# Feed-forward norm and output projection by halves, the gate projection z at the end of the preceding pass, weights by one branch, and a new order of calls

## The chip, the cores and the metric

The kernel runs on 1 core of one Trainium2 chip. The metric is the device time in microseconds (us) of one execution, the median of several runs.

## The reference

Sixteen sequences of 512 tokens with 256 features pass through two layers. Layer 0 is attention and a feed-forward part, layer 1 a selective scan and a small quantised linear map. Each part stands behind a layer norm, with shift, scale and gate (`sa, ca, ga, sb, cb, gb`) from a conditioning vector.

```python
# layer 0
h = _layernorm(x) * (1 + ca) + sa
q, k, v = heads of h @ W.T (16 heads of 16), q and k normed per head
x = x + ga * (softmax(causal(q k^T / 4)) v) @ Wu.T
h = _layernorm(x) * (1 + cb) + sb
t = silu(tlin(h, w1)) * tlin(h, w2)            # 256 -> 1024
t = gelu(tlin(t, h1)); t = gelu(tlin(t, h2))   # 1024 -> 1024, twice
x = x + gb * tlin(t, w3)                       # 1024 -> 256
# layer 1
h = _layernorm(x) * (1 + ca) + sa
xp, z = split(h @ W_in)                        # 256 -> 2 x 512
dlt, Bm, Cm = split(xp @ W_xproj)
delta = clip(softplus(dlt @ W_dt + b_dt), 0.001, 0.1)
for each token: s = (1 + A * delta) * s + Bm * delta * xp; y = sum(Cm * s)   # 16 states
x = x + ga * ((y + D * xp) * silu(z)) @ W_out
h = _layernorm(x) * (1 + cb) + sb
x = x + gb * (quantise(h, blocks of 32) @ quantise(W).T + bias)
```

## The kernel before

**Passes.** One pass works on up to three sequences at once, in stages that the engines interleave. `att` and `ffn` are layer 0 of sequence b, `pre` is layer 1 up to the scans of states 0 to 11 for b-1, and `fin` is the rest of layer 1 for b-2: the scans of states 12 to 15, the gate, the output projection and the quantised linear map. `Pass` says which parts are on. The program is: a set-up; pass 0 (attention alone, which also splits the weights); the feed-forward of sequence 0 with pass 1; a loop of two turns over seven unrolled steady passes with all parts on (14 passes); and two last passes without layer 0. A steady pass begins here where the last feed-forward product `mid(17)` of the one before ends on PE.

**Order.** The order of the work on each engine is written out by hand, as a list of calls at the end of `tensor_pass`, `scalar_pass`, `vector_pass` and `gpsimd_pass`. Engines run their lists strictly in order and wait on semaphores, so a call that waits holds everything behind it. What depends on the part of the pass:

- *Attention*, four quads of heads with three groups each: `scores` (PE) to `find_max` (DVE, L1988) to `turn_max` (PE) to `shift_q` (DVE, L1995) to `scores_turned` (PE, L1131) to `exp_probs` (ACT, L1569) to `causal_probs` (POOL) to `values` (PE) to `row_sums`, `invert_sums`, `weigh` (DVE, L2000). `att_proj` (PE, L1162) and `att_add` (DVE) close it.
- *Gate projection z*: `gate_in(m)` (PE, L1006, four of two matmuls each), `gate_silu(m)` (ACT, L1521) into `z_s`, then `gate_out` (POOL, L714), which multiplies the scan's sum, and `out_proj` (PE, L1043). It reads the normed input `h3` of the pass before, so it has to stand ahead of `pre_affine`, which overwrites `h3`.
- *Layer 1*: `in_proj`, `x_proj`, `dt_proj` (PE), `dt_bias`, `softplus` (ACT), `clip_dt` (DVE, L2017), then for each state a decay (ACT), a product with B, a scan and a product with C (DVE), and an addition (POOL). States 12 to 15 are `tail_*`, 0 and 1 `head_*`, both beside the attention; 2 to 11 (`times_b`, `scan`, `times_c`) run beside the feed-forward.
- *Feed-forward norm*: `ffn_mean` (PE), `ffn_centre` (DVE, L229), `ffn_square` (ACT, L238), `ffn_var` (PE, L223), `ffn_rstd` (ACT, a Ln L242 and an Exp L244), `ffn_scale` (DVE, L233), `ffn_affine` (ACT, L1404: for each half of the features a value rounded to fp32r and a full one), `split_h` (POOL: the difference of the two). Each of centre, square and scale is one instruction over both halves.
- *Feed-forward*: every weight product is two fp32r matmuls (high and low part of the activations) of 0.23 us; `up(n)` waits for rounded and split input together. `up_gate` is a Silu (ACT, L1412), `gate_up` (DVE, L1940) the product, `gelu` (L1425).

**Weights.** Pass 0 rounds each of 22 weight tiles to fp32r (`split_act`), computes what rounding left (`split_dve`: a difference L451 and its largest value L453), and stores both, as `w_hi` and `w_lo`. `find_flag` then puts into `has_rest` whether anything was left. The weights of the reference are -1, 0 and 1, so nothing is. Each product asks `has_rest` by a branch (L918) of its own, 34 in a pass; the block that it jumps over holds 4 or 16 matmuls.

**Activation tables.** Silu, Gelu, and Ln with Exp stand in different table sets of ACT. `preload_act_table_set(LN_EXP)` at L1454 and L1523 loads the set that has both Ln and Exp; elsewhere the program gets a load where a function is not in the set that is loaded. A steady pass has five loads: before `gate_silu(0)`, after `gate_silu(3)`, before `up_gate(0)`, before `gelu(0)` and before `next_rstd`.

## Time and profile before

| | us |
|---|---|
| Median of 3 runs | 4162.34 (4157.99 to 4164.06) |
| The profiled execution, its own time | 4167.61 |
| Its span, first to last instruction | 4165.8 |
| PE busy, DVE busy | 3523.9 (85%), 3318.2 (80%) |
| POOL busy, ACT busy | 2716.0 (65%), 2583.4 (62%) |

The span is the time from the first to the last instruction. An engine's busy time is the sum of its instructions. In a timeline a row is one instruction or a run of equal ones: start and duration in us, the number behind x, and in brackets how long the engine stood idle before it and which work it waited for. An fp32 matmul shows as two rows of matmuls, so x4 is two matmuls. The steady passes follow each other every 235.5 us, and the rows below are from one of them.

### The profile page before, as it was taken

Reading aid. Unit: us, or ns where it says so; the run is one execution under the profiler, and the core shown is the slowest. Engines: PE = TensorE matmul, PEld = TensorE weight load, DVE = VectorE, ACT = ScalarE, POOL = GpSimd, SP = SyncE. Lnnn points to the kernel's source line nnn. Section 1 sums busy time; section 2 is a strip of 40 time slices with the busy share of each in tenths; the row PEclk is TensorE's granted clock in tenths of the full one; section 3 lists DMA queues with packets and bytes.
Section 4 is the critical chain, followed back from the end, with each engine's and each line's share of the span. In section 5 each row is a group of like instructions: output and inputs, shape, how many; then the busy total and the mean of one; then the engine's idle time right before and its main releaser. Section 6 shows DMA issues by size and latency. Waiting matters only on the chain. (4 is left out here: it accounts for less than half of the span.)

```text
span 4165.8 us, 50421 instructions
## 1 busy us (share of the span) xinstructions
PE 3523.9 (85%) x16621; PEld 2034.0 (49%) x16621; DVE 3318.2 (80%) x3646; ACT 2583.4 (62%) x3703; POOL 2716.0 (65%) x1960
## 2 busy tenths in 40 slices
PE   5687888989899998989898898989999898989513
PEld 3263645546373645546373554636364554636201
DVE  4514878989798888979797887979898897979694
ACT  2345566767667676766666676767667676666431
POOL 0132866768595876768595776759586776768563
PEclk9799999999999999999999999999999999999756
DMA  4630201102030301103030211203030211203000
GB/s 164 258 105 15 97 21 62 62 26 97 6 117 1 97 26 61 62 21 102 6 102 17 82 41 46 77 8 115 1 107 16 76 46 41 82 6 102 0 5 5
DMA packets 69435, 247.81 MB, mean 59 GB/s; under 512 B 9472, under 2 KB 10112, under 8 KB 68736
## 3 DMA queue, kind: packets, MB, share of 16 engines
q1 hardware_dynamic: 66816, 235.35, 16.8%
q10 hardware_dynamic: 2304, 8.39, 0.5%
q8 instruction: 182, 2.98, 0.3%
q14 instruction: 133, 1.09, 0.1%
HBM read 212.25 MB, written 31.46 MB: 59 GB/s over the span
## 5 line engine op out<-in xcount | busy, mean ns | idle before, releaser
L671 POOL TENSOR_TENSOR kept<-kept,hb 128x512 f32<-128x512 f32 x640 | 811.0, 1300 | 71.1 <-DVE hb L1925 70.9
L1916 DVE TENSOR_TENSOR_SCAN hb<-ps,hb 128x512 f32<-128x512 f32 x640 | 745.0, 1205 | 17.5 <-ACT ps L1362 12.7
L929 PE MATMUL ps<-hid_bhi,wring 128*128 128x512 f32 x1536 | 628.0, 409 | 70.9 <-issue 53.6
L929 PE MATMUL ps<-hid_blo,wring 128*128 128x512 f32 x1536 | 619.8, 404 | 0.0
L1362 ACT ACTIVATE ps<-kept,a_neg 128x512 f32<-128x512 f32 x640 | 423.0, 690 | 174.4 <-DVE hb L1916 174.4
L929 PE MATMUL ps<-hid_ahi,wring 128*128 128x512 f32 x1280 | 516.7, 404 | 8.0 <-POOL hid_alo L686 8.0
L639 POOL TENSOR_TENSOR kept<-kept,hb 128x1024 f32<-128x1024 f32 x128 | 300.2, 2360 | 336.3 <-DVE hb L1860 297.7
L929 PE MATMUL ps<-hid_alo,wring 128*128 128x512 f32 x1280 | 505.0, 395 | 0.0
L632 POOL TENSOR_SCALAR_AFFINE_SELECT room<-room 128x512 f32<-128x512 f32 x256 | 217.7, 862 | 427.2 <-ACT room L1569 427.2
L1988 DVE TENSOR_REDUCE room<-ps 128x4 f32<-128x2048 f32 (+3 forms) x256 | 375.2, 1486 | 123.6 <-PE ps L1105 111.3
L1925 DVE TENSOR_TENSOR hb<-hb,ps 128x512 f32<-128x512 f32 x640 | 404.0, 673 | 0.1
L1569 ACT ACTIVATE room<-ps 128x2048 f32<-128x2048 f32 (+1 forms) x192 | 304.8, 1588 | 155.2 <-PE ps L1131 155.1
L929 PEld LDWEIGHTS ps<-hid_bhi,wring 128*128 128x128 f32 x1536 | 298.4, 194 | 173.8 <-issue 73.5
L929 PEld LDWEIGHTS ps<-hid_blo,wring 128*128 128x128 f32 x1536 | 297.9, 194 | 67.4
L1853 DVE TENSOR_TENSOR_SCAN hb<-hb 128x1024 f32<-128x1024 f32 x128 | 319.4, 2505 | 10.1 <-POOL hb L696 4.1
L1905 DVE TENSOR_TENSOR hb<-kept,ps 128x512 f32<-128x512 f32 x480 | 305.1, 676 | 12.0 <-POOL kept L648 9.0
L929 PEld LDWEIGHTS ps<-hid_ahi,wring 128*128 128x128 f32 x1280 | 240.6, 188 | 84.5 <-POOL hid_alo L686 19.9
L1103 PE MATMUL ps<-room 32*128 32x512 f32 (+3 forms) x2048 | 216.3, 492 | 72.2 <-ACT room L1569 52.3
L929 PEld LDWEIGHTS ps<-hid_alo,wring 128*128 128x128 f32 x1280 | 240.7, 188 | 58.3 <-issue 4.1
L1131 PE MATMUL ps<-room 32*128 32x512 f32 (+3 forms) x2048 | 214.0, 512 | 44.0 <-DVE room L1988 29.0
L648 POOL TENSOR_TENSOR kept<-kept,hb 128x1024 f32<-128x1024 f32 x64 | 150.8, 2356 | 135.8 <-DVE hb L1887 134.5
L686 POOL TENSOR_TENSOR hid_alo<-ln_s,hid_ahi 128x512 fp32r<-128x512 f32 x128 | 167.5, 1308 | 78.4 <-ACT hid_ahi L1417 68.6
(198 smaller groups left out, 7359.2 us busy)
## 6 DMA issues: line engine op xcount, KB each, us to landing
wring<-w_hi SPq DMA_DIRECT2D x352, 512.0 KB, 3.3
kept<-in_wffn SPq DMA_DIRECT2D x22, 512.0 KB, 6.3
w_hi<-wring SPq DMA_DIRECT2D x22, 512.0 KB, 7.0
w_lo<-wrest SPq DMA_DIRECT2D x22, 512.0 KB, 5.2
xn<-in_x_fm SPq DMA_DIRECT2D x17, 512.0 KB, 3.3
out_fm<-xc ACTq DMA_DIRECT2D x16, 512.0 KB, 5.4
room<-in_wmod SPq DMA_DIRECT2D x2, 1536.0 KB, 8.1
win<-in_win SPq DMA_DIRECT2D x1, 1024.0 KB, 8.4
```

The costliest lines, as they stand in the source:

```text
L632: pool.affine_select(blk, blk, [[0, 4], [1, P]], ALU.is_ge, 0.0, base=0, channel_multiplier=-1).then_inc(p_masked, 1)
L639: pool.tensor_tensor(pair_of(acc, h), pair_of(acc, h), pair_of(hb, h), ALU.add).then_inc(tail_acc, 2)
L671: pool.tensor_tensor(acc[:, m, :], acc[:, m, :], hb[:, s % 8, :], ALU.add).then_inc(acc_done, 1)
L929: mm = pe.matmul(bank(bk), wring[:, r % 3, at + k * P:at + (k + 1) * P], src[i][:, k, :], start=(k == 0 and i == 0), stop=(k == K - 1 and ...
L1103: pe.matmul(bank(g)[:, at:at + w], q_ver[r, p, c, i * P:(i + 1) * P], k_ver[r, p, c, 0:w], start=True, stop=False)
L1362: act.activation(bank(2 + m % 2), dt[:, m, :], ACT.Identity, bias=1.0, scale=a_neg[:, m, n:n + 1]).then_inc(a_ready, 1)
L1569: act.activation(probs[u], ps[:, 0:4, 0:G_WIDTH[u]], ACT.Exp).then_inc(exp_done, 1)
L1853: dve.tensor_tensor_scan(both, pair_of(hb, 2 + h).rearrange("p a t -> p (a t)"), both, 0.0, ALU.mult, ALU.add).then_inc(tail_scanned, 2)
L1905: dve.tensor_tensor(hb[:, s % 8, :], u[:, m, :], bank(0), ALU.mult).then_inc(b_ready, 1)
L1916: dve.tensor_tensor_scan(hb[:, s % 8, :], bank(2 + m % 2), hb[:, s % 8, :], 0.0, ALU.mult, ALU.add).then_inc(scanned, 1)
L1925: dve.tensor_tensor(hb[:, s % 8, :], hb[:, s % 8, :], bank(1), ALU.mult).then_inc(y_ready, 1)
L1988: ins = dve.tensor_reduce(cols, ps[:, 0:4, at:at + (i + 1) * P], AX.X, ALU.max, negate=True)
```

## The change

1. **z one pass earlier.** `gate_in` and `gate_silu` move from `fin` to `pre`: they work on the `h3` of their own pass, at the end of its attention, and use banks 2 and 3. The products 0 and 1 are copied out (`copy_z`), and their Silu is one instruction of 1024 columns in the middle of the gelus (`gate_silu_copied`); 2 and 3 go through Silu at once. `decay(2, .)`, which uses the same banks, waits for them. `qk_rs` and `next_log` move out of the memory that `z_s` now holds for longer.
2. **Halves.** The feed-forward norm's centre, square, variance, scale and affine work by halves, with semaphores of their own. `att_proj` is cut into single matmuls. The first two up products are cut into a high part, which waits for the rounded input alone, and a low part.
3. **Weights.** The rest is computed in place of the loaded tile and only measured; `w_lo` is gone, with its 22 stores. If `has_rest` is set, the raw weights are used in fp32. One branch per pass on PE and on SP chooses between two whole copies of the feed-forward's list.
4. **Order.** The four lists of calls are in another order throughout.

```diff
         def split_act(act, t):
...
+                    act.wait_ge(w_split, t - 2)
...
-                dve.tensor_tensor(wrest[:, t % 2, :], stage[:, t % 3, :], wring[:, t % 3, :].bitcast(F32), ALU.subtract).then_inc(w_split, 1)
+                dve.tensor_tensor(stage[:, t % 3, :], stage[:, t % 3, :], wring[:, t % 3, :].bitcast(F32), ALU.subtract).then_inc(w_split, 1)
...
-            def up(n):
+            def up_high(n, exact):
                 if ffn:
...
+                    pe.wait_ge(h_rounded, since(h_rounded, DC))
+                    wait_tile(0, exact)
...
+                    up_product(n, 0, exact)
+
+            def up_low(n, exact):
+                if ffn:
+                    pe.wait_ge(h_split, since(h_split, DC))
+                    up_product(n, 1, exact).then_inc(up_done, 1)
...
             def gate_in(m):
-                if fin:
+                if pre:
                     if m >= 2:
-                        pe.wait_ge(z_ready, since(z_ready, m - 1))
-                    elif pre:
-                        pe.wait_ge((ln_cent, ln_norm)[m], k_pre.number)
+                        pe.wait_ge(z_copied, since(z_copied, m - 1))
+                    else:
+                        pe.wait_ge(scanned, since(scanned, 0))
+                        if att:
+                            pe.wait_ge(exp_done, since(exp_done, 3 * QUADS))
...
+            if ffn:
+                with pe.If(has_rest > 0):
+                    feed_forward(False)
+                with pe.Else():
+                    feed_forward(True)
...
+            def ffn_rstd():
                 if ffn:
-                    act_rstd(act, k_ffn, 4)
...
+                    act.wait_ge(f_var, since(f_var, 1))
+                    act.activation(ln_s[:, 0, :], bank(4), ACT.Ln, bias=eps[:, 0:1]).then_inc(f_log, 1)
+                    act.wait_ge(f_log, since(f_log, 1))
+                    act.activation(bank(4), ln_s[:, 0, :], ACT.Exp, scale=-0.5).then_inc(f_rstd, 1)
...
+            def copy_z(m):
+                if pre:
+                    act.wait_ge(z_done, since(z_done, m + 1))
+                    if fin:
+                        act.wait_ge(quantised, since(quantised, 2 * QN - 1))
+                    act.activation(z_s[:, m, :], bank(2 + m), ACT.Copy).then_inc(z_copied, 1)
...
+            def gate_silu_copied():
+                if pre:
+                    act.wait_ge(z_copied, since(z_copied, 2))
+                    act.activation(pair_of(z_s, 0), pair_of(z_s, 0), ACT.Silu).then_inc(z_ready, 2)
...
+            def ffn_centre(c):
                 if ffn:
...
+                    dve.tensor_tensor(ln_x[:, c, :], xa[:, c, :], bank(4), ALU.subtract).then_inc(f_cent, 1)
```

**PE, early in a steady pass**, from the first turned scores of quad 0. L855 is a row of B or C for the tail scans, L1103 and L1105 are scores, L1131 turned scores, L1006 the gate projection and L1018 `in_proj`. Before:

```order
L1131 MATMUL ps<-room 128x512 x4
L1006 MATMUL ps<-kept,win 128x512 x2
L855 MATMUL ps<-bc_parts,bc_sel 128x512
L1103 MATMUL ps<-room 128x384 x4
L1105 MATMUL ps<-causal_r,ident_r 128x128 x4
L1103 MATMUL ps<-room 128x128 x4
L1105 MATMUL ps<-causal_r,ident_r 128x128 x4
L1006 MATMUL ps<-kept,win 128x512 x4
L855 MATMUL ps<-bc_parts,bc_sel 128x512
L1006 MATMUL ps<-kept,win 128x512 x2
L1131 MATMUL ps<-room 128x384 x4
L1131 MATMUL ps<-room 128x128 x4
```

The changed kernel, where L848 is the row for the scans, L1122 and L1124 are scores, L1150 turned scores and L1037 `in_proj`:

```order
L1150 MATMUL ps<-room 128x512 x4
L848 MATMUL ps<-bc_parts,bc_sel 128x512
L1122 MATMUL ps<-room 128x384 x4
L1124 MATMUL ps<-causal_r,ident_r 128x128 x4
L1122 MATMUL ps<-room 128x128 x4
L1124 MATMUL ps<-causal_r,ident_r 128x128 x4
L1037 MATMUL ps<-kept,win 128x512 x2
L848 MATMUL ps<-bc_parts,bc_sel 128x512
L1037 MATMUL ps<-kept,win 128x512 x2
L848 MATMUL ps<-bc_parts,bc_sel 128x512
L1150 MATMUL ps<-room 128x384 x4
L1150 MATMUL ps<-room 128x128 x4
```

The eight gate matmuls are gone from this place, and the `in_proj` matmuls have moved up into it, each behind its row for the tail scans.

**PE, from the row sums of the last quad to the feed-forward.** L1154 is `row_sums(3)`, L1162 `att_proj`, L1070 `fin_back`, L217 and L223 mean and variance, L1078 `fin_ff`, L884 the rows for state 2. Before:

```order
L1154 MATMUL ps<-room,sum_sel 128x512
L1162 MATMUL ps<-room,wu 128x512 x6
L1070 MATMUL ps<-ident,room 128x128 x8
L217 MATMUL ps<-xa,mean_mat 128x512 x2
L884 MATMUL ps<-bc_parts,bc_sel 128x512
L223 MATMUL ps<-ln_s,mean_mat 128x512 x2
L1078 MATMUL ps<-room,wdq 128x512 x2
L884 MATMUL ps<-bc_parts,bc_sel 128x512
L1078 MATMUL ps<-room,wdq 128x512 x2
L929 MATMUL ps<-hid_bhi,wring 128x512
L929 MATMUL ps<-hid_blo,wring 128x512
L918 COMPARE_AND_BRANCH
```

The changed kernel from `fin_back(1)` on (L883 and L891 are mean and variance, L1027 the gate projection, L1097 `fin_ff`, L877 the rows for state 2):

```order
L1089 MATMUL ps<-ident,room 128x128 x4
L883 MATMUL ps<-xa,mean_mat 128x512 x2
L1027 MATMUL ps<-kept,win 128x512 x2
L891 MATMUL ps<-ln_s,mean_mat 128x512 x2
L877 MATMUL ps<-bc_parts,bc_sel 128x512
L1097 MATMUL ps<-room,wdq 128x512 x2
L1027 MATMUL ps<-kept,win 128x512 x2
L877 MATMUL ps<-bc_parts,bc_sel 128x512
L1097 MATMUL ps<-room,wdq 128x512 x2
L1340 COMPARE_AND_BRANCH
```

Gate projections 2 and 3 stand between mean and variance and between the two `fin_ff`; 0 and 1 stand ahead of this place. The branch L1340 skips the whole raw copy of the feed-forward, which stands right behind it: 352 fp32 matmuls of weights, and what stands between them.

**ACT, the feed-forward's norm.** L238 is the square, L1616 `fin_cols`, L1386 `copy_b`, L242 and L244 Ln and Exp, L1404 the affine, L1412 `up_gate(0)`. Before:

```order
L1362 ACTIVATE ps<-kept,a_neg 128x512 x2
L238 ACTIVATE ln_s<-ln_x 128x1024
L1616 ACTIVATE room<-ps 128x2x256 x2
L1386 ACTIVATE b_rows<-ps 128x512
L242 ACTIVATE ln_s<-ps,eps 128x512
L244 ACTIVATE ps<-ln_s 128x512
L1404 ACTIVATE hid_bhi<-ln_x,m 128x512
L1404 ACTIVATE h_ln<-ln_x,m 128x512
L1404 ACTIVATE hid_bhi<-ln_x,m 128x512
L1404 ACTIVATE h_ln<-ln_x,m 128x512
L1412 ACT_TABLE_LOAD
L1412 ACTIVATE ln_x<-ps,s 128x512
```

The changed kernel, behind the two squares (L1567 is `gate_silu`, L1430 and L1432 Ln and Exp, L1420 `copy_b`, L1440 the affine, L1396 `decay`):

```order
L1567 ACT_TABLE_LOAD
L1567 ACTIVATE room<-ps 128x512
L1430 ACT_TABLE_LOAD
L1430 ACTIVATE ln_s<-ps,eps 128x512
L1432 ACT_TABLE_LOAD
L1432 ACTIVATE ps<-ln_s 128x512
L1420 ACTIVATE b_rows<-ps 128x512
L1440 ACTIVATE hid_bhi<-ln_x,m 128x512
L1440 ACTIVATE h_ln<-ln_x,m 128x512 x2
L1440 ACTIVATE hid_bhi<-ln_x,m 128x512
L1567 ACT_TABLE_LOAD
L1567 ACTIVATE room<-ps 128x512
```

Four table loads stand in the changed rows, before `gate_silu(2)`, the Ln, the Exp and `gate_silu(3)`, where one stood before. A steady pass has eight loads instead of five.

## Rows read from the trace of the kernel before

**Rows 1.** The page: the span, and busy time of each engine.

```profile
span 4165.8 us, 50421 instructions
PE 3523.9 (85%) x16621; PEld 2034.0 (49%) x16621; DVE 3318.2 (80%) x3646; ACT 2583.4 (62%) x3703; POOL 2716.0 (65%) x1960
```

**Rows 2.** Stretches of one steady pass: engines' busy time, clock, DMA.

```profile
core 0: us, PE busy (x) PEld busy (x) DVE busy (x) ACT busy (x) POOL busy (x), PEclk, DMA share, GB/s
2662.50:2710.40 47.90, 43.16 (x204) 19.80 (x204) 40.41 (x38) 36.98 (x52) 26.88 (x18) 1.00 0.09 34
2710.40:2745.00 34.60, 32.91 (x205) 13.56 (x205) 25.55 (x19) 22.53 (x28) 27.25 (x16) 1.00 0.00 1
2745.00:2793.00 48.00, 41.20 (x236) 17.42 (x234) 36.43 (x44) 27.00 (x35) 22.35 (x18) 0.86 0.02 6
2793.00:2805.00 12.00, 6.36 (x16) 2.88 (x15) 10.36 (x10) 8.02 (x11) 6.42 (x5) 0.98 0.06 25
2805.00:2888.00 83.00, 81.77 (x340) 64.06 (x340) 79.38 (x102) 56.95 (x94) 76.69 (x61) 0.98 0.39 128
2888.00:2898.00 10.00, 10.00 (x39) 6.96 (x37) 9.70 (x14) 7.52 (x11) 9.88 (x8) 1.00 0.01 2
```

**Rows 3.** Timeline of PE, the gate projections of one pass.

```profile
2694.07 1.98 PE L1006 MATMUL ps<-kept,win 128*128 128x512 f32 x4
2698.13 3.65 PE L1006 MATMUL ps<-kept,win 128*128 128x512 f32 x8
2702.14 1.88 PE L1006 MATMUL ps<-kept,win 128*128 128x512 f32 x4
```

**Rows 4.** Timeline of DVE, first half of the pass.

```profile
2670.07 0.69 DVE L1978 TENSOR_TENSOR room<-ps,room 128x512 f32<-128x512 f32 x1 [3.50 <-ACT room L1489]
2734.61 1.23 DVE L1988 TENSOR_REDUCE room<-ps 128x4 f32<-128x1024 f32 x1 [2.43 <-PE ps L1105]
2737.97 1.36 DVE L2017 TENSOR_SCALAR kept<-kept 128x2048 f32<-128x2048 f32 x1 [2.13 <-ACT kept L1560]
2741.31 0.69 DVE L1995 TENSOR_TENSOR room<-room,ps 128x512 f32<-128x512 f32 x1 [1.98 <-PE ps L1114]
```

**Rows 5.** Timeline of PE, the output projection of the pass.

```profile
2737.13 3.70 PE L1043 MATMUL ps<-kept,wout 128*128 128x512 f32 x8 [0.49 <-POOL kept L714]
```

**Rows 6.** Timeline of DVE, second half of the attention.

```profile
2762.54 0.69 DVE L262 TENSOR_REDUCE q_am<-room 128x16 f32<-128x512 f32 x1 [1.95 <-ACT room L1610]
2776.43 0.69 DVE L262 TENSOR_REDUCE q_am<-room 128x16 f32<-128x512 f32 x1 [3.63 <-ACT room L1610]
2793.06 1.22 DVE L229 TENSOR_TENSOR ln_x<-xa,ps 128x1024 f32<-128x1024 f32 x1 [2.08 <-PE ps L217]
```

**Rows 7.** Timeline of ACT, the feed-forward's norm and first gate.

```profile
2794.32 1.06 ACT L238 ACTIVATE ln_s<-ln_x 128x1024 f32<-128x1024 f32 x1 [6.78 <-DVE ln_x L229]
2797.45 0.69 ACT L242 ACTIVATE ln_s<-ps,eps 128x512 f32<-128x512 f32 x1 [0.62 <-PE ps L223]
2798.16 0.60 ACT L244 ACTIVATE ps<-ln_s 128x512 f32<-128x512 f32 x1
2803.05 1.28 ACT L1412 ACT_TABLE_LOAD   x1
2808.18 0.69 ACT L1412 ACTIVATE ln_x<-ps,s 128x512 f32<-128x512 f32 x1 [3.85 <-PE ps L929]
```

**Rows 8.** Timeline of PE, the first matmul of the feed-forward.

```profile
2804.54 0.77 PE L929 MATMUL ps<-hid_bhi,wring 128*128 128x512 f32 x1 [3.47 <-issue]
```

**Rows 9.** Branches of PE's sequencer, by line: ns min/median/max.

```profile
L918 PEldq COMPARE_BRANCH  x544: 202/208/367, 221.3 to 3834.8; - x182
L2269 PEldq COMPARE_BRANCH  x2: 79/1775/3471, 2192.3 to 3847.8; - x2
```

**Rows 10.** Waits of 60 to 215 us; DVE's work for one weight tile.

```profile
ACT wring L444 <- DMA kept<-in_wffn: 37.6, 16, 3.8
L453 DVE TENSOR_REDUCE rest_max<-wrest 128x1 f32<-128x1024 f32 x22 | 26.8, 1220 | 0.8
```

More of the change, by code:

```diff
@@ L1252, in tensor_pass @@
             values(3, 2)
+            att_proj(1, 0)
+            att_proj(1, 1)
+            att_proj(2, 0)
             row_sums(3)
[L1254 to L1257 removed]
+            gate_in(1)
+            att_proj(2, 1)
+            att_proj(3, 0)
+            att_proj(3, 1)
             fin_back(1)
[L1259 removed]
+            ffn_mean(0)
+            ffn_mean(1)
+            gate_in(2)
+            ffn_var(0)
+            ffn_var(1)
```

675 lines of the change are left out of this document (343 added, 332 removed).

## The prediction

> **What bounds the kernel now.** I read the page first. PE is busy for 85% of the span and DVE for 80% [rows 1], so neither alone sets the time, and a mean over stages says little. The steady passes hold most of it: 14 of 235.5 us, 3297 of 4165.8 us. So I cut one of them into stretches [rows 2]; its DVE busy time sums to 201.8 us and its PE busy time to 215.4, so that 33.7 and 20.1 us of idle time are all that an order of calls can win. In the last two stretches, the feed-forward, PE has 91.8 of 93 us and DVE 89.1: both are full, and nothing is to be won. In the first, DVE works 40.4 of 47.9 us, and 3.50 of its idle time is the start of the pass, where it waits for the first q [rows 4]. In the second, PE is full (32.9 of 34.6) and DVE idles for 9.0 us; three of its waits are 2.43 us for the last scores of quad 2, 2.13 for softplus and 1.98 for the turned maxima [rows 4]. In the third neither is full, and DVE waits 1.95 and 3.63 us for rows to quantise [rows 6]. The fourth is the feed-forward's norm: PE works 6.4 of 12 us.
>
> **The change, part by part, for a steady pass.** Times are counted from the row of the pass's norm where I name no other.
>
> *z leaves the early part.* Four gate projections take 1.98, 3.65 and 1.88 us on PE, 7.5 together [rows 3]. ACT also loses four Silus and two table loads of 1.28 us (one stands in [rows 7]). In the first stretch this buys nothing: DVE is the fuller engine beside its 3.50 us at the start, and that wait hangs on `project`, `square` and `head_rstd`, which all stay. Moreover the new order puts the C row of tail state 2 ahead of turned scores, and that row waits for `tail_in(2,0)` on DVE; I expect PE to stand idle there instead of multiplying. The second stretch is where it pays. PE enters it with `in_proj(2)` done (1.9 us less to do), and DVE runs `tail_out(3,1)` before `split_bc` and `find_max(2,1)`, 0.7 and 2.4 us earlier, so that POOL finishes `gate_out` some 3 us earlier; `out_proj(0)` waited for it by 0.49 us after PE had got there [rows 5]. The waits of 2.43, 2.13 and 1.98 us then shrink. Bounds: nothing (DVE keeps waiting for other things), and all 6.5 us. I take the middle, 3.4 us less.
>
> *Second half of the attention.* `fin_turn(1)` and `fin_rows(1)` stand one group of scores further ahead, so the wait of 3.63 us goes; `weigh(1)` moves into the wait of 1.95. Against it `gate_in(0)` and `gate_in(1)` are on PE here, 1.9 us each; PE has 6.8 us idle in this stretch (48 less 41.2), but `gate_in(0)` stands ahead of the last values, with ACT's invert and DVE's `weigh(3)` queued behind them. Working the rows through in the new order, DVE waits some 2.6 us before `weigh(2)` and 2 before `weigh(3)` instead. `att_proj` by single matmuls and `fin_back(0)` ahead of it let the mean follow the last addition directly, where DVE had waited for it (third row of [rows 6]). Bounds: 0 and 5.6 us (both waits gone). I take 3.1 us less.
>
> *The norm.* Before, the centre starts at 0 (2793.06), the square ends at 2.3, Ln starts at 4.4, Exp ends at 5.7, the last affine ends at 10.0 [rows 6, 7], and the first feed-forward matmul starts at 11.5 [rows 8]. After, the halves bring the squares to 1.9, and the variance, now behind `gate_in(2)`, to 3.5. But ACT's list is then: table load to 3.2, `gate_silu(2)` to 3.8, table load to 5.1, Ln to 5.8, table load to 7.1, Exp to 7.7. That is 2.0 us later than before. The scale by halves lets the affine start at 8.4 and end at 11.4; `up_high(0)` needs no split and starts at 11.5, as before. Then ACT loads Silu again and does `gate_silu(3)`, `decay(2,0)` and `copy_b(3)`, and reaches `up_gate(0)` at 15.1, where it stood before (2808.18) [rows 7]. DVE waits for `decay(2,0)`, which once was long done, and is about 1.8 us behind when it has done `gate_up(1)` and `scan(2,1)`. At the other end of the feed-forward `ffn_add(1)` stands 2.3 us of scans further ahead on DVE and covers this, and PE is not late. So the cost lies between 0 and 1.8 us; I take 1.0. The two loads and the Silu of 1024 columns amid the gelus stand before `decay(8,1)`. ACT is busy 57 of 83 us there, and DVE has 4 us of products to do meanwhile: nothing. If that cover went, it would cost 3.6 us a pass (two loads of 1.28, and 1.06 as the square of 1024 columns).
>
> *One branch instead of 34.* The short ones take 0.208 us each, beside running matmuls: removing them gives nothing. A long one is the jump back at the end of the loop's body, taken once, with 3.47 us; the other of its two executions, with 0.08, is the one that leaves the loop [rows 9]. The new branch jumps over 352 fp32 matmuls of weights, and which of 0.21 and 3.47 us it takes no row shows. I take 3.47, nearer in kind. It starts when `fin_ff(1)` is handed to PE, at about 8.3, and ends at 11.8, when `up_high(0)` could start at 11.5; `up_low(0)` waits to 12.6 for the split anyway. So 0 to 0.5 us, within the 1.0 above.
>
> The Trainium skill (Runtime: NRT & Kernel Launch, Instruction fetch mechanics) says that a taken branch whose target lies outside the two pages of instructions at hand stops for a fetch. The jump back agrees, with its 3.47 us, and so do the short ones; by that rule alone, with nothing hidden, the sum would be that of rival 3.
>
> *Sum of a steady pass*: -3.4 - 3.1 + 1.0 = -5.5 us; 14 passes: -77.
>
> *Pass 0.* ACT waits 37.6 us for weight tiles to be loaded [rows 10]. Each tile made three transfers of 512 KB, and now makes two. A third of the waiting is 12.5 us. Each tile also costs DVE two instructions of 1.22 us [rows 10], which stay, and ACT now waits for the difference too. Bounds 0 and 25; I take -11. *Feed-forward of sequence 0 and pass 1*: the halves without the extra Silu, -2, and -1. The last two passes: Silu goes, `decay(2,0)` waits for z; nothing.
>
> Together -91: 4167.6 - 91 = 4076.6. The profiled execution was 5.3 us above the median of the runs shown (4162.3), so I forecast **4071 us**, 2.2% less.
>
> **The rivals.**
>
> 1. *DVE takes the gain back (4120 us).* The waits of rows 4 and 6 are DVE's, but the order is tight, and a wait removed returns two calls later for another engine. For it: DVE's 84% in the first stretch. Against: PE's full second stretch. If only 2 us a pass remain of the 6.5, the pass is 2 less 1.0 for the norm shorter, 14 us in all, and 14 for the rest: 4134; with 3 us remaining, 4120.
> 2. *Slower: the table loads (4190 us).* Place: ACT between the square and `up_gate(0)`. Price: Exp 2.0 us later, and 3.2 us of load, Silu and decay ahead of `up_gate(0)`. If neither halves nor the boundary cover them and they also push DVE's scans, a pass is 5.2 us longer; with 2 us won earlier it is 3.2 longer, +45 in 14 passes, -14 for the start: 4193. It decides from the point where less than 5.2 us is won before the norm. Against: the scale and affine by halves, of which the rows show the sizes.
> 3. *The long branch is not hidden (4119 us).* Place: PE before `up_high(0)`. If `fin_ff(1)` is handed over late or the fetch goes on behind the jump, 3 of 3.47 us are seen in each of 16 feed-forwards: +48.
> 4. *More than forecast (4015 us).* All waits of rows 4 and 6 go, and with PE's gaps filled the clock of 0.86 in the third stretch [rows 2] rises towards 1. Then -9.5 a pass.
> 5. *The measured z move does nothing and only the start-up gains (4150 us)*: as rival 1 with nothing left.
>
> **How the numbers follow.** Forecast 0.52, with its own range 4030 to 4100; rival 1 0.15, rival 2 0.11, rival 3 0.10, rival 4 0.08, rival 5 0.04. The range 4010 to 4145 holds the forecast, rivals 1, 3 and 4 for the most part, and leaves out rival 2 and half of 5. A difference under 0.2%, 8 us, is about what a measurement of this kernel cannot tell from none. Faster: everything but rival 2 and part of 5, 0.85; within 0.2%, 0.04; slower 0.11.
>
> **What the profile would show.** Steady passes of about 230 us; PE's gate projections in gaps behind the last exponentials; no wait of 3.6 us before the second quantisation, but new ones before `weigh(2)` and `weigh(3)`; `out_proj(0)` some 3 us earlier in the pass; four table loads around the norm, Exp ending 7.7 us after the centre starts, the first feed-forward matmul still near 11.5; one long branch per pass on PE of some 3.5 us; the feed-forward from there to the last matmul as long as now; pass 0 shorter by 11 us. I would be wrong if the first stretch grew by PE standing behind the C row, if Exp ended later than 9, or if PE's first feed-forward matmul came after 13.

## The result, and the profile after

The changed kernel takes **4278.88 us** (median of 4 runs, 4276.42 to 4283.32); the kernel before, with its fourth run, 4163.2. The ratio is 1.0274, with a 95% interval of 1.025 to 1.0299: **2.7% slower**, where I forecast 2.2% faster. The time even lies above the rival for a slower kernel (4190). The profiled execution took 4279.24 us, 111.6 more than the one of before.

The page, as [rows 1]:

```profile
span 4277.5 us, 49727 instructions
PE 3510.6 (82%) x16621; PEld 2021.0 (47%) x16621; DVE 3388.6 (79%) x3678; ACT 2666.1 (62%) x3780; POOL 2694.8 (63%) x1960
```

PE has the same 16621 matmuls and is busy less. DVE has 32 instructions more but is busy for 70 us more: some of its instructions take longer than they did. The 111.6 us lie as follows, by the start of the feed-forward norm's centre in each pass: 12.0 before the first centre (220.3 against 208.3 us), 7.5 and 11.6 in the next two passes, 74.6 in twelve steady passes (5.2 to 8.3 each), 11.4 in the pass in which the loop turns, and 5.4 less in the end.

The stretches of one steady pass of 242 us (the last matmul of `mid(17)` of the pass ahead starts at 2749.9, the centre at 2886.4). The first two rows are as long as those of [rows 2], the next two go on to the centre, and the last is 83 us of the feed-forward:

```profile
core 0: us, PE busy (x) PEld busy (x) DVE busy (x) ACT busy (x) POOL busy (x), PEclk, DMA share, GB/s
2749.90:2797.80 47.90, 37.17 (x180) 16.85 (x179) 43.55 (x39) 34.56 (x50) 28.42 (x18) 1.00 0.10 33
2797.80:2832.40 34.60, 26.90 (x171) 10.18 (x169) 24.22 (x17) 17.68 (x24) 19.26 (x11) 0.95 0.00 0
2832.40:2874.40 42.00, 35.23 (x239) 15.33 (x239) 31.94 (x34) 28.03 (x34) 23.36 (x19) 1.00 0.00 1
2874.40:2886.40 12.00, 12.00 (x59) 5.54 (x52) 9.29 (x14) 3.89 (x7) 5.68 (x3) 1.00 0.03 6
2898.00:2981.00 83.00, 80.52 (x337) 62.47 (x338) 78.88 (x101) 62.54 (x98) 77.16 (x62) 1.00 0.36 121
```

Read PE first. In the first two stretches it works 64.1 us, where before it worked 76.1 [rows 2]; only 7.5 of these 12 are the gate products. The rest, 4.5 us, is work that it has not reached, though it stands idle for 7.7 of the 34.6 us of the second stretch. DVE is a little busier than before in these two stretches together (67.8 us for 66.0), though it gets less far. The next rows say how far.

The following table is the base of all that follows. It counts us from the start of the last feed-forward matmul of the pass ahead to the start of four maxima of the attention on DVE, and to the norm's centre. Each is the median over the 12 steady passes away from the loop's turn. The experiments below are in it, but for e7, whose figures are those of the changed kernel.

| | find_max(1,0) | (2,0) | (2,2) | (3,2) | centre | (3,2) to centre |
|---|---|---|---|---|---|---|
| before | 28.2 | 56.1 | 72.5 | 97.2 | 130.9 | 33.7 |
| after | 31.2 | 58.9 | 79.7 | 105.2 | 135.6 | 30.4 |
| e1 first half as before | 28.7 | 58.3 | 75.1 | 101.1 | 131.5 | 30.4 |
| e2 DVE and POOL only | 33.1 | 65.5 | 87.9 | 113.3 | 143.7 | 30.4 |
| e3 PE and ACT only | 36.5 | 72.0 | 89.7 | 115.2 | 145.6 | 30.4 |
| e4 after, POOL fills | 31.2 | 56.7 | 77.5 | 103.0 | 133.3 | 30.4 |
| e5 e1, z back too | 28.7 | 56.6 | 73.0 | 99.1 | 128.7 | 29.6 |
| e6 e1, PE filled | 28.7 | 56.4 | 72.8 | 98.9 | 129.2 | 30.4 |
| e8 before, POOL fills | 28.2 | 56.0 | 72.3 | 96.4 | 128.4 | 32.0 |
| e9 after, three calls moved | 31.2 | 59.9 | 79.7 | 106.8 | 137.2 | 30.4 |
| e10 after, PE filled | 31.2 | 59.3 | 80.1 | 105.6 | 135.9 | 30.4 |
| e11 e5, second half as before | 28.7 | 56.6 | 73.0 | 97.8 | 127.4 | 29.6 |
| e12 e5, row copied sooner | 28.7 | 56.6 | 73.0 | 99.1 | 127.5 | 28.4 |
| e13 e6, new order in quad 0 | 31.2 | 58.0 | 74.5 | 100.5 | 130.9 | 30.4 |
| e14 after, old order in quad 0 | 28.7 | 57.8 | 78.6 | 104.1 | 134.5 | 30.4 |
| e15 e12, calls up to find_max(3,2) as before | 28.7 | 56.6 | 73.0 | 97.8 | 127.4 | 29.6 |
| e16 e6, new order from quad 2 | 28.7 | 56.4 | 75.3 | 100.8 | 131.2 | 30.4 |

So the first half of the attention (up to find_max(3,2)) is 8.0 us longer, the second (from there to the centre) 3.3 us shorter, and norm and feed-forward 0.7 us longer (centre to first matmul 11.56 for 11.48, first to last 93.8 for 93.2). The second and third figures are nearly those of my sum (-3.1 and +1.0). **The first is its failure: -3.4 forecast, +8.0 measured.**

The timeline of DVE in this pass, with the stretched instructions and the waits that answer to [rows 4]:

```profile
2755.70 2.16 DVE L1872 COPY m<-mod 128x12 f32 x3
...
2794.98 4.28 DVE L1909 TENSOR_TENSOR_SCAN hb<-hb 128x1024 f32<-128x1024 f32 x1
...
2801.66 3.58 DVE L1909 TENSOR_TENSOR_SCAN hb<-hb 128x1024 f32<-128x1024 f32 x1
...
2809.72 2.29 DVE L2047 TENSOR_REDUCE room<-ps 128x4 f32<-128x2048 f32 x1 [2.54 <-PE ps L1124]
...
2830.50 1.23 DVE L2047 TENSOR_REDUCE room<-ps 128x4 f32<-128x1024 f32 x1 [4.30 <-PE ps L1124]
...
2834.13 1.23 DVE L2076 TENSOR_SCALAR kept<-kept 128x2048 f32<-128x2048 f32 x1 [2.40 <-ACT kept L1611]
```

The timeline of POOL beside it:

```profile
2788.03 6.54 POOL L632 TENSOR_TENSOR kept<-kept,hb 128x1024 f32<-128x1024 f32 x2 [0.67 <-DVE hb L1916]
2794.75 2.36 POOL L689 TENSOR_TENSOR hb<-kept,b_rows 128x1024 f32<-128x1024 f32 x1 [0.17 <-POOL kept L632]
...
2800.75 2.34 POOL L632 TENSOR_TENSOR kept<-kept,hb 128x1024 f32<-128x1024 f32 x1 [0.47 <-DVE hb L1916]
```

A tail scan of 1024 columns takes 2.28 us alone. The first here overlaps 2.13 us of POOL's product, which started first, and takes 2.0 us more; the second overlaps 1.43 us of an addition and takes 1.30 more. Where the scan started first (2787.81, 2.28 us), POOL's two additions took 6.54 us instead of some 4.7. Over the whole program the 192 tail and head scans take 73.1 us more than 2.283 each, where before they took 32.6. This sum is called the scans' excess below. The three copies of 12 columns, 0.32 us in the pass of before, now start 0.4 us behind POOL's last two additions (2755.33, 2.50 us), end with them, and take 2.16. That costs little: find_max(0,0) comes at 13.2 us of this pass and at 13.0 of the one before, since the copies end within what was a wait of 3.50 us [rows 4].

The timeline of PE, the waits in the same stretch:

```profile
2791.51 0.50 PE L848 MATMUL ps<-bc_parts,bc_sel 128*128 128x512 f32 x1 [1.01 <-DVE hb L1916]
...
2794.90 0.50 PE L848 MATMUL ps<-bc_parts,bc_sel 128*128 128x512 f32 x1 [1.18 <-DVE hb L1900]
...
2801.80 0.71 PE L1150 MATMUL ps<-room 32*128 32x256 f32 x8 [2.22 <-DVE room L2047]
...
2806.64 0.50 PE L848 MATMUL ps<-bc_parts,bc_sel 128*128 128x512 f32 x1 [1.78 <-DVE hb L1916]
```

PE stands behind B and C rows (L848) and turned scores (L1150) that wait for DVE, 6.2 us in four waits. At the same place before stood gate products, which wait for nothing there.

The norm went as forecast. Timeline of ACT, as [rows 7], then PE, as [rows 8], then the branch over all passes, as [rows 9]:

```profile
2888.33 1.28 ACT L1567 ACT_TABLE_LOAD   x1
...
2890.24 1.28 ACT L1430 ACT_TABLE_LOAD   x1
...
2892.24 1.28 ACT L1432 ACT_TABLE_LOAD   x1
2893.53 0.60 ACT L1432 ACTIVATE ps<-ln_s 128x512 f32<-128x512 f32 x1
```

```profile
2897.92 1.20 PE L941 MATMUL ps<-hid_bhi,wring 128*128 128x512 f32 x4 [2.50 <-ACT hid_bhi L1440]
```

```profile
L1340 PEldq COMPARE_BRANCH  x16: 3316/3380/3797, 222.4 to 3854.6; - x16
```

The Exp ends 7.77 us after the centre (forecast 7.7), the first matmul starts 11.56 after it (11.5), and the long branch takes 3.38 us (3.47). It starts 2.4 us after the centre (2888.8), not 8.3, and is over before anyone could want PE: PE's wait is for ACT's rounded input.

### The profile page after: what moved, and what is told of

It reads as the page before. It is cut to its first block and busy times, and to the rows that moved or that the text cites. A ratio compares the mean times of both kernels' runs of the same rounds, so it can differ in the third digit from the quotient of the medians.

```text
span 4277.5 us, 49727 instructions
## 1 busy us (share of the span) xinstructions
PE 3510.6 (82%) x16621; PEld 2021.0 (47%) x16621; DVE 3388.6 (79%) x3678; ACT 2666.1 (62%) x3780; POOL 2694.8 (63%) x1960
## 5 line engine op out<-in xcount | busy, mean ns | idle before, releaser
L930 PE MATMUL ps<-hid_bhi,wring 128*128 128x512 f32 x1408 | 560.6, 398 | 18.6 <-DVE h_ln L1999 11.0
L1396 ACT ACTIVATE ps<-kept,a_neg 128x512 f32<-128x512 f32 x640 | 428.3, 696 | 233.5 <-DVE hb L1972 233.4
L930 PE MATMUL ps<-hid_blo,wring 128*128 128x512 f32 x1408 | 555.4, 394 | 0.0
L632 POOL TENSOR_TENSOR kept<-kept,hb 128x1024 f32<-128x1024 f32 x128 | 329.4, 2590 | 264.4 <-DVE hb L1916 206.2
L625 POOL TENSOR_SCALAR_AFFINE_SELECT room<-room 128x512 f32<-128x512 f32 x256 | 192.7, 770 | 423.9 <-ACT room L1620 422.1
L1909 DVE TENSOR_TENSOR_SCAN hb<-hb 128x1024 f32<-128x1024 f32 x128 | 344.4, 2702 | 9.0 <-POOL hb L689 4.1
L1122 PE MATMUL ps<-room 32*128 32x512 f32 (+3 forms) x2048 | 226.5, 513 | 139.5 <-ACT room L1620 73.9
L1150 PE MATMUL ps<-room 32*128 32x512 f32 (+3 forms) x2048 | 201.6, 487 | 136.8 <-DVE room L2047 100.1
L930 PEld LDWEIGHTS ps<-hid_bhi,wring 128*128 128x128 f32 x1408 | 264.3, 188 | 96.8 <-DVE ln_s L1999 17.8
L930 PEld LDWEIGHTS ps<-hid_blo,wring 128*128 128x128 f32 x1408 | 264.4, 188 | 60.5
L641 POOL TENSOR_TENSOR kept<-kept,hb 128x1024 f32<-128x1024 f32 x64 | 152.5, 2383 | 166.5 <-DVE hb L1943 161.9
L653 POOL TENSOR_TENSOR hb<-kept,b_rows 128x512 f32<-128x512 f32 x160 | 207.7, 1298 | 33.4 <-ACT b_rows L1420 31.1
```

The source lines that it names most:

```text
L632: pool.tensor_tensor(pair_of(acc, h), pair_of(acc, h), pair_of(hb, h), ALU.add).then_inc(tail_acc, 2)
L653: pool.tensor_tensor(hb[:, s % 8, :], u[:, m, :], b_rows[:, n % 2, :], ALU.mult).then_inc(b_by_pool, 1)
L930: mm = pe.matmul(bank(bk), w, x, start=(k == 0 and i == 0), stop=(k == K - 1 and i == 1))
L1122: pe.matmul(bank(g)[:, at:at + w], q_ver[r, p, c, i * P:(i + 1) * P], k_ver[r, p, c, 0:w], start=True, stop=False)
L1396: act.activation(bank(2 + m % 2), dt[:, m, :], ACT.Identity, bias=1.0, scale=a_neg[:, m, n:n + 1]).then_inc(a_ready, 1)
L1909: dve.tensor_tensor_scan(both, pair_of(hb, 2 + h).rearrange("p a t -> p (a t)"), both, 0.0, ALU.mult, ALU.add).then_inc(tail_scanned, 2)
```

## The experiments

**The first half in the order of before (e1).** The lists of all four engines up to `out_proj(0)`, `exp_probs(1,2)`, `shift_q(2)` and `causal_probs(1,2)` are those of before, without gate calls. A piece of PE's:

```diff
             scores_turned(0, 0)
             tail_spread(1, 1)
             scores(1, 1)
-            in_proj(0)
             tail_spread(0, 2)
-            in_proj(1)
-            tail_spread(1, 2)
             scores_turned(0, 1)
+            tail_spread(1, 2)
+            in_proj(0)
+            in_proj(1)
+            scores(1, 2)
             in_proj(2)
-            scores(1, 2)
             scores_turned(0, 2)
```

> The changed kernel with the first part of the attention in the order of before on PE, ACT, DVE and POOL (without the gate projections, which stay at the pass's end); all else is the change's. In a steady pass of the changed kernel the stretch from the last feed-forward product to the centre of the norm is 4.7 us longer than before, and all of that and more (9.2 us) has grown by the time of find_max(3,2); the second half is 3.3 us shorter. Theory A (the fitted order makes POOL's long products meet DVE's scans and copies, which then take longer: 4.28, 3.58 and 3.24 us where 2.28 is usual) and theory B (PE stands behind rows of the tail scans and behind scores, which wait for DVE) both expect the 9.2 us back: a period of about 232 us, 4150 us in all. Theory C (the moved gate, the new places of buffers or the copies of the program, not the order, made the stretch longer) expects 4260 to 4280.

4200.7 us, 1.0076 of before (1.0049 to 1.0103). The order made 78 of the 112 us: 4.1 a pass in the first half, and 16 before the first centre (204.3 us). Theory C falls as the whole cause, but 3.9 of the 8.0 us stay, where theories A and B expected none. Part of them is in this row of the windows and in these of PE's timeline:

```profile
2952.00:2983.00 31.00, 23.81 (x133) 10.52 (x132) 26.20 (x20) 14.84 (x19) 17.96 (x11) 0.78 0.00 1
```

```profile
2966.89 0.80 PE L848 MATMUL ps<-bc_parts,bc_sel 128*128 128x512 f32 x1 [2.56 <-DVE hb L1916]
2969.16 2.09 PE L1150 MATMUL ps<-room 32*128 32x384 f32 x16 [1.47 <-DVE room L2047]
2971.18 0.80 PE L848 MATMUL ps<-bc_parts,bc_sel 128*128 128x512 f32 x1
2971.77 5.50 PE L1037 MATMUL ps<-kept,win 128*128 128x512 f32 x8
```

The gate products, eight fp32 matmuls, had stood where PE now waits. The granted clock is 1.00 up to 2961.9 us and 0.50, the lower of PE's two levels (1.2 of 2.4 GHz), from 2962.0 to 2975.5; in the 17 us before it fell PE had worked 13.8. `in_proj(0)` and `(1)` take 5.50 us there, where eight such matmuls took 3.70 [rows 5].

**Two engines at a time (e2, e3).** The same edit on two engines' lists only.

> The same part in the order of before on DVE and POOL alone; PE and ACT keep the new order. Theory A expects nearly all of the gain of the first experiment, about 4170 us, with scans of 2.28 us again. Theory B expects less than half of it, 4220 us or more, with PE still waiting in front of the rows for the tail scans.

> The same part in the order of before on PE and ACT alone; DVE and POOL keep the new order. Theory A expects little, 4250 to 4280 us. Theory B expects most of the gain, about 4180 us. If neither alone gives half of it, the orders of the four engines only work as a set.

4399.7 and 4407.2 us (1.0554 and 1.0573). Neither theory forecast this, and the third case, that the orders only work as a set, had no price: each half of the edit makes the kernel 120 to 130 us slower, both together 78 faster. A list of calls is only right against the other three; from these two runs nothing can be told about which engine's order is at fault. They do tell that the scans' excess does not rank the kernels: it is 53 and 52 us here, less than the changed kernel's 73.

**PE filled (e6).** On top of e1, at the four old places of the gate products:

```diff
+            def fill_pe(m):
+                if fin:
+                    if m < 2 and pre:
+                        pe.wait_ge((ln_cent, ln_norm)[m], k_pre.number)
+                    for c in range(DC):
+                        pe.matmul(bank((FB, FA)[m % 2]), win[:, c, m * P:(m + 1) * P], win[:, c, :T], start=(c == 0), stop=(c == DC - 1))
```

> As the first experiment, and eight fp32 matmuls on constant weights, whose result nobody reads, stand on PE where the gate products of before stood; they replace nothing and no ACT work comes with them. Theory D expects in_proj 0 and 1 at full clock again, find_max(1,2) some 3 us earlier than in the first experiment, and 4150 to 4165 us in all, faster with 7.5 us more work on PE. Rival E expects it slower than the first experiment (4201), by up to 7.5 us a pass, or the same.

4168.3 us (1.0005, 0.9988 to 1.0021): **7.5 us more matmuls a pass, whose result nobody reads, make the kernel 32 us faster than e1.** The windows row of the same stretch and two rows of PE:

```profile
2930.40:2961.40 31.00, 29.37 (x172) 12.49 (x172) 28.11 (x22) 17.37 (x24) 21.06 (x12) 1.00 0.00 1
```

```profile
2945.62 1.88 PE L1036 MATMUL ps<-win 128*128 128x512 f32 x4
...
2949.02 3.59 PE L1044 MATMUL ps<-kept,win 128*128 128x512 f32 x8
```

The clock is 1.00, and 2.2 us a pass come back. Nothing else was changed, so it is shown that in the old order the gate products' place was worth more than their time.

**z back in its place (e5).** On top of e1, gate projection and Silus stand and work as before; copies, `gate_silu_copied` and `decay`'s wait are gone.

```diff
             scores_turned(0, 0)
+            gate_in(0)
             tail_spread(1, 1)
             scores(1, 1)
+            gate_in(1)
+            gate_in(2)
             tail_spread(0, 2)
+            gate_in(3)
...
             def gate_in(m):
-                if pre:
+                if fin:
```

> As the first experiment, and the gate projection z and its Silus stand where before had them too (early in the pass, on the old input, in the old banks; no copies of z). What is left of the change: the norm, output projection and first products by halves, the weights by one branch, the second half's order and the feed-forward's. In the first experiment PE stood idle where the four gate products had been, its granted clock fell to 0.78 of full speed over 31 us, and in_proj 0 and 1 took 5.50 us instead of 3.70, so that find_max(1,2) came 3.4 us later than before. Theory D (the gate products were useful filling: without them PE idles behind DVE and its clock falls) expects this stretch as before, the second half still 3 us shorter, and a norm some 2 us shorter, since its three table loads of 1.28 us are gone: a period of 230 to 231 us against 235.5, 4085 us in all. Rival E (PE's work is too long there: taking out 7.5 us helps, and it is DVE's waits that moved) expects a stretch no shorter than that of the first experiment, 4170 us.

4101.7 us, **0.9837 of before (0.9802 to 0.9871)**. That is 17 us more than expected; find_max(3,2) still comes 1.9 us later than before. The first matmul starts 8.60 us after the centre, 2.9 us sooner than before and 3.0 sooner than after. ACT in its norm (the centre started at 2751.65), then PE:

```profile
2755.14 0.69 ACT L1430 ACTIVATE ln_s<-ps,eps 128x512 f32<-128x512 f32 x1 [1.54 <-PE ps L890]
2755.86 0.60 ACT L1432 ACTIVATE ps<-ln_s 128x512 f32<-128x512 f32 x1
```

```profile
2760.25 1.19 PE L940 MATMUL ps<-hid_bhi,wring 128*128 128x512 f32 x4 [1.25 <-ACT hid_bhi L1440]
```

The norm's part of the change (the halves, with the first products cut in two; no run takes them apart) is worth 2.9 us a pass here, and the late z took all of it. From e6 to e5 it is 67 us: a pass is 3.0 us shorter from centre to first matmul, 1.0 in the feed-forward and 0.5 ahead of the centre.

**One table load less (e7).** One line ahead of the norm's Ln in the changed kernel: `act.preload_act_table_set(LN_EXP)`.

> The changed kernel with one line more: the table set that has both Ln and Exp is loaded ahead of the norm's Ln, so that one load stands there instead of two. If the norm's chain hangs on ACT's loads as I predicted, the Exp ends 1.3 us earlier, the first feed-forward matmul starts 10.3 us after the centre instead of 11.6, and the time falls by 16 times 1.3 us, to 4260. If another work (the branch of 3.3 us, or fin_ff on PE) is next to it, the first matmul stays near 11.6 and so does the time.

4257.7 us. The first matmul starts 10.28 us after the centre: 1.28 less, 21 us in all. The chain over ACT is the one that decides there, and a load on it costs its full length.

**POOL's reads taken away (e4, e8).** In both kernels:

```diff
+            def fill(dst, pair, sem, inc):
+                lo, hi = dst[:, 2 * pair, :], dst[:, 2 * pair + 1, :]
+                pool.memset(lo.bitcast(mybir.dt.bfloat16), 0.0)
+                pool.memset(hi[:, :T // 2].bitcast(mybir.dt.bfloat16), 0.0)
+                pool.memset(hi[:, T // 2:].bitcast(mybir.dt.uint8), 0).then_inc(sem, inc)
...
-                    pool.tensor_tensor(pair_of(acc, h), pair_of(acc, h), pair_of(hb, h), ALU.add).then_inc(tail_acc, 2)
+                    fill(acc, h, tail_acc, 2)
```

> The changed kernel, in which POOL's 1024-column products and additions of the attention (tail and head products with B, additions to the sum, the gate, dt times x) are left out and replaced by fills of the same outputs with zero, in three pieces of about the same length in all; fills read nothing. The scan's values are then zero; every wait stays. Theory A: DVE's tail and head scans all take 2.28 us, 73 us less on DVE in 192 scans, and the time falls by 50 us or more, to 4230 or less. Theory B: the scans' length was covered by DVE's other waits and the time falls by less than 20 us.

> The kernel before with POOL's 1024-column work of the attention replaced by fills of zero, as in the fourth experiment (which leaves the scan's values zero). There DVE's 192 long scans lost 73 us of excess over 2.28 us each, and the time 41 us. Here the excess is 33 us. If a stretched scan costs the same share here, the time falls by some 18 us, to 4149, and the meetings of POOL and DVE explain 20 to 25 us of the 112; if it falls by 40 us too, what e4 gained was POOL's own work or something else that both kernels have.

4238.2 and 4135.0 us: 41 us less in the changed kernel, between what the two theories expected, and 28 to 31 less in the one of before, where I had expected 18. Groups by form of e4:

```profile
L1915 DVE TENSOR_TENSOR_SCAN hb<-hb 128x1024 f32<-128x1024 f32 x128 | 290.8, 2283 | 4.9 <-ACT hb L1378 0.2
...
L1942 DVE TENSOR_TENSOR_SCAN hb<-hb 128x1024 f32<-128x1024 f32 x64 | 146.1, 2283 | 2.6 <-POOL hb L685 2.4
...
L685 POOL MEMSET kept<- 128x1024 uint8 x256 | 244.0, 953 | 0.0
L683 POOL MEMSET kept<- 128x1024 bf16 x256 | 243.7, 952 | 517.6 <-DVE hb L1922 257.0 <-DVE kept L2082 100.6 <-DVE hb L1949 99.0
```

Every scan of e4 takes 2.26 to 2.29 us beside a POOL that writes and doesn't read. This is the rule of the Trainium skill (SBUF — State Buffer, Who interferes with whom): a DVE instruction with two SBUF inputs contends with a GpSimd instruction that reads SBUF, not with one that only writes, and which was issued first decides who blocks. The trace agrees in both directions, with the scans of 4.28 us and the additions of 6.54. In the table the fills move find_max(3,2) by 2.2 us in the changed kernel and 0.8 in that of before: the meetings of these scans explain some **1.4 of the 8.0 us** (the small copies keep theirs in both runs). In whole times the difference is 10 to 13 of the 112 us, since the fills also shorten the second half of the kernel before by 1.7 us a pass, and do not in the changed one. Theory A is a real mechanism and a small part.

**Local repairs in the new order (e9, e10).** e9 moves three calls:

```diff
-            find_max(2, 0)
             tail_in(3, 0)
+            find_max(2, 0)
...
-            values(1, 0)
-            dt_proj(3)
             scores(2, 2)
+            dt_proj(3)
+            values(1, 0)
```

> The changed kernel with three calls of the attention's first part moved: on DVE tail_in(3,0) ahead of find_max(2,0), as before had it, and on PE values(1,0) and dt_proj(3) behind scores(2,2). In the changed kernel DVE waits 2.54 us for the scores ahead of find_max(2,0) and 4.30 us ahead of find_max(2,2), for which PE had other products in its list first. Theory B (calls in the wrong place for what DVE and PE have to give each other) expects 1 to 2.5 us a pass back, 4240 to 4265 us in all. If the same time only reappears at the next wait, it stays within 5 us of 4279.

e10 puts three fillings ahead of PE's waits in the new order.

> The changed kernel in its own order, with three products on constant weights (six fp32 matmuls, 5.6 us of PE a pass, read by nobody) ahead of three places where PE stands: tail_spread(0,2), scores_turned(0,2) and tail_spread(0,3). There the granted clock is 0.96 in the first 48 us of the pass and 0.90 in the next 34.5. Theory D expects the clock near 1 and 1 to 3 us a pass less, 4235 to 4265 us. If the clock costs nothing in this order because DVE is the bound there, the time stays or rises, by up to 5 us a pass.

4295.9 and 4286.3 us: both slower than the changed kernel (4278.9), both misses. In e9 the scans' excess rose from 73.1 to 84.9 us; moving three calls out of two conspicuous waits made others. In e10 two things got better and the time did not: over the 34.6 us of the second stretch the granted clock rose from 0.95 to 1.00 (medians of twelve passes), the scans' excess fell from 73.1 to 55.9 us, and find_max(3,2) still came at 105.6 us for 105.2. So in the new order the clock is not what is short. e10 also bounds theory D: filling paid where the clock had fallen far (0.78 over 31 us in e1), not wherever PE waits.

**The second half as before (e11).** On top of e5, with lists up to `fin_back(1)`, `invert_sums(3)`, `att_add(1)` and `head_add(1,1)`.

```diff
+            values(1, 1)
             scores(3, 0)
             out_proj(1)
...
-            fin_turn(1)
             values(2, 1)
             scores_turned(3, 1)
...
             row_sums(2)
+            fin_turn(1)
```

> The fifth experiment (first half and z as before), with the second half of the attention, from out_proj(0) to the last output projection, in the order of before too. What then is left of the change: the halves, the weights by one branch, and the feed-forward's order. I had forecast 3.1 us a pass from the second half's order, and the two kernels differ there by 3.3. If that is the order's doing, this takes 3 to 4 us a pass more than the fifth experiment: 4145 to 4160 us. If the gain came from the halves instead, it stays near 4102.

4108.5 us (0.9857, 0.984 to 0.9873), 7 us more than e5, where 43 to 58 more were expected: the order that I had credited with 3.1 us a pass is worth 0.9 behind find_max(3,2) (29.6 for 30.5 us in the mean of twelve passes), and loses 1.3 ahead of it. The reason is in the kernel before. In its passes 2 and 3 and at the loop's turn this part takes 29.6 us, not 33.7; timeline and windows of pass 2:

```profile
654.88 0.69 DVE L262 TENSOR_REDUCE q_am<-room 128x16 f32<-128x512 f32 x1 [1.33 <-ACT room L1610]
```

```profile
643.00:670.00 27.00, 21.98 (x146) 9.57 (x145) 21.66 (x32) 13.53 (x18) 13.16 (x12) 1.00 0.02 3
```

With the clock at 1.00 the wait is 1.33 us; it is 3.4 to 3.63 in the eleven passes where the clock from find_max(3,2) to the centre is 0.80 to 0.89 [rows 2, 6]. e11 does both: 29.3 us in seven of its fourteen passes, with the clock at 1.00, and 30.4 to 33.5 in the others, at 0.80 to 0.94. The changed kernel and e5 have it at 1.00 in every pass, and take 30.4 and 29.6 us. So the 3.3 us of the second half are the clock's, and what the new order does there is to keep it: e5 and e11 differ in nothing but this order.

**Where in the first half (e13, e14, e16).** The new order up to `scores(1,0)` only, everywhere but there, and only from `scores(2,0)` on.

> The sixth experiment (first half as before, PE filled), with the new order on all four engines up to scores(1,0) and find_max(1,0) only. Read from the two traces, the new order is 3.0 us behind there (31.2 against 28.2 us after the last feed-forward product). If the parts add up, find_max(3,2) comes 3 us later than in the sixth experiment (98.9), the pass is 3 us longer, and the time 45 us more: 4213 us. If DVE's and PE's later waits absorb it, 4170 to 4185.

> The changed kernel, with the order of before up to the same place only. If the parts add up, the pass is 3 us shorter than the changed kernel's, 4234 us in all. If the 6.3 us come from what follows, it stays above 4265.

> The sixth experiment, with the new order only from scores(2,0) and find_max(2,0) to out_proj(0): tail_out(3,1), head_spread(0,0), row_sums(0) and values(1,0) sooner, and dt_proj and scores in another mix. Between find_max(2,0) and find_max(2,2) the new order needs 20.8 us and the old one 16.4. If this stretch's own order costs that, the pass is 3 to 4 us longer than the sixth's and the time 4215 to 4230. If the stretch is only slow because PE comes to it with work left over (in_proj 3, values 0) and the wrong clock, it stays near 4168.

4203.7, 4256.6 and 4200.7 us, each between the two times that I had named for it. From e6 (98.9 us at find_max(3,2)), the new order of quad 0 costs 1.6, that from quad 2 on 1.9 us. The changed kernel is 6.3 us behind e6, so 2.8 more belong to quad 1, to what the parts do together, or to the filling, which e6, e13 and e16 have and the changed kernel lacks (filled in other places it is 6.7 behind, e10). The scans' excess is 35.7 us in e6, 36.0 in e13, 53.2 in e16 and 71.5 in e14: the order of quad 0 costs its 1.6 us without it.

**A faster version (e12, e15).** DVE waits 2.22 us in e5 for ACT's copy of a row that PE made some 4 us sooner. e12:

```diff
+            copy_head(1)
             exp_probs(3, 2)
             invert_sums(2)
-            copy_head(1)
```

> The fifth experiment with one call moved on ACT: copy_head(1), the row of B for head state 1, ahead of exp_probs(3,2). DVE waits 2.22 us for that copy in head_in(1,0), though PE's row is ready 4 to 5 us sooner. If the end of the attention hangs on DVE, which is busy from there to weigh(3), the pass is up to 2.2 us shorter: 4070 us. If it hangs on PE, ACT and the last exponentials, the wait moves to weigh(2) or weigh(3) and the time stays near 4102.

> The twelfth experiment with the calls between out_proj(0) and find_max(3,2) in the order of before on all four engines (values(1,1) ahead of scores(3,0), values(1,2) ahead of fin_var). The eleventh reached find_max(3,2) at 97.8 us where the fifth and twelfth need 99.1, and the twelfth takes 28.4 us from there to the centre at full clock. If both hold together the pass is 1.3 us shorter than the twelfth's: 4065 us. If the clock falls in the second half as it did in half of the eleventh's passes, 4086 or more.

e15 is e12 with the calls between `out_proj(0)` and find_max(3,2) in the order of before. e12 takes **4085.9 us, 0.9798 of before (0.9782 to 0.9814)**, where up to 2.2 us a pass (4070) were hoped for; e15 4084.5 (0.981, 0.9794 to 0.9826), no better within the noise. Of the 2.22 us 1.2 a pass arrive; DVE's `head_in(1,0)` in e12 follows at once, and the next wait is 0.52:

```profile
2953.88 1.16 DVE L1931 TENSOR_TENSOR hb<-kept,ps 128x1024 f32<-128x1024 f32 x1
2955.57 0.69 DVE L2063 TENSOR_TENSOR room<-room,ps 128x512 f32<-128x512 f32 x1 [0.52 <-ACT ps L1637]
```

In e15 the 1.3 us won ahead of find_max(3,2) are given back behind it (29.6 for 28.4): the granted clock is 0.94 of full speed in that stretch in most passes, and 0.84 in the two where it takes 31.5 and 31.7 us.

## Why the prediction was wrong

1. *The early part: wrong.* The step that failed is "z leaves the early part": in the first stretch this "buys nothing", and "the second stretch is where it pays", -3.4 us. Measured +8.0 at find_max(3,2). By the experiments it is a sum, taken in this order: +1.7 from before to e6, +2.2 because in the old order the gate products no longer keep PE busy and its clock up (e6 to e1), +4.1 for the new order (e1 to after). Taken the other way the second term is not there: in the new order a filling of six matmuls at other places bought nothing (e10). Of the first term 0.5 are there at find_max(0,0) (13.6 us for 13.0), where in e5 a copy of 12 columns takes 1.26 us beside POOL's product, and some 1.3 come from the calls between `out_proj(0)` and find_max(3,2) (e5 to e11). I had seen PE stand behind the C row, had written that it would "stand idle there instead of multiplying", and had even named it as a sign of being wrong. I priced the idleness at nothing because DVE was "the fuller engine"; by [rows 2] PE was the busier one there, 43.2 of 47.9 us against 40.4. The row on PE gates DVE's scans, and by the end of the second stretch 4.5 us of PE's work were left over, with a wait of 4.30 us ahead of find_max(2,2).
2. *Durations taken as fixed: wrong.* I carried DVE's scans at 2.28 us into an order in which they meet POOL's products, though two scans of before, in one row of 5.69 us, showed such a meeting. Worth some 1.4 us a pass.
3. *Second half: right in size (-3.3 for -3.1), wrong in mechanism.* I gave it to two waits that the new order shortens. The wait of 3.63 us was long because the clock had fallen; e11 keeps the old order and has the gain wherever the clock holds. The new order gains by keeping the clock, which I had not reckoned with, so that the size came out right is luck. What I gave rival 4 (a clock near 1 in the third stretch) is what came.
4. *Norm and first products: right.* Exp at 7.77 for 7.7, first matmul at 11.56 for 11.5, +0.7 us a pass for +1.0. The branch is long (3.38 for 3.47 us) and hidden: rival 3 did not come. e7 confirms the price of a load on this chain.
5. *Pass 0: wrong.* I took -11 for the missing third of the weight transfers. The wait for tiles fell from 37.6 [rows 10] to 34.1 us only, and the first centre came 12.0 us later. In pass 0 the new lists have ACT's first rounding at 88.3 us instead of 78.8, and the load of the third tile is issued at 89.7 us instead of 67.0:

```profile
ACT wring L442 <- DMA kept<-in_wffn: 34.1, 16, 4.3
```

With the old lists of the first half (e1) that load is issued at 80.2 us and the first centre comes at 204.3 us, 4.0 sooner than before. That is what is left of my 11. With them on PE and ACT alone (e3) it comes at 210.7, on DVE and POOL alone (e2) at 222.4, so the late start is in the lists of PE and ACT. The feed-forward of sequence 0 and pass 1, for which I had -3, took 7.5 us more.
6. *Not in my sum: the passes in which the kernel before kept its clock.* In the turning pass the stretch to the centre is 149.3 us long instead of 138.6, 6.0 more than a steady pass's 4.7. DVE's last instruction of the block ends 5.8 us after the last feed-forward matmul's start (4.4 before), and PE's jump back took 4.36 us instead of 3.47; find_max(1,0) is 2.0 us further behind than in a steady pass. Most of the rest is that before took 29.6 us from find_max(3,2) to the centre in this pass, with its clock at 1.00, so that the 3.3 us of item 3 are not won (30.4 for 29.6). So it is in passes 2 and 3, in which before has 29.6 too: they are 11.6 and 8.3 us longer after the change, the other steady passes 5.2 to 6.5.
7. *The rivals.* Rival 2 had the sign, but with table loads as its mechanism, and these cost 0.7 us a pass net. None of mine said that taking work from PE could slow PE.

What stays open: how most of the new order's cost in the first half arises. The scans' meetings are 1.4 us of it and the clock is not it (e10), 1.6 and 1.9 us sit in quad 0 and from quad 2 on, and 2.8 are not placed. Open is also why the clock holds with one order of the second half and not with the other. No edit here tells these apart.

## What to carry to other kernels

A product that fills a wait may not be worth its duration when it is moved: look at what stands beside it, and whether PE's granted clock hangs on it. An order of calls fitted on fixed durations must be held against the instructions that take longer together (here DVE's two-input scans and POOL's long products), and here it could not be repaired engine by engine: half an order was worse than either whole. And a wait in the trace may be a fallen clock: compare the same wait in a pass that has the full one, before counting it as winnable.

## What the runs showed of the hardware

- Matmuls without use paid: 7.5 us of them a pass took 32 us off the program, with the granted clock of a 31 us stretch going from 0.78 to 1.00.
- Copies of 12 columns on DVE, 0.16 us alone, took up to 1.26 us beside POOL's additions and products and up to 2.2 us beside its fills (three of them from 2267.3 us on in the changed kernel), which do not hold up the scans.
- Fills of 128x1024 on POOL took 0.95 us in bf16 and in uint8 and 0.96 in fp32, one of 128x512 in bf16 0.53 (e4): there they went by elements, not by bytes.
- The same list of calls gave stretches of two lengths within one execution: e11's second half took 29.3 us with the granted clock at 1.00, and up to 33.5 with it at 0.80.
